# Four PSUM banks in turn, and one signal for two visits, in the segment sum of a graph layer

## What is computed

```python
msg = x @ M
agg = jax.ops.segment_sum(msg[edge_src], edge_dst, num_segments=x.shape[0])
return jax.nn.relu(self_term + agg)          # self_term = x @ W
```

```python
for ei in range(NUM_EXPERTS):
    g = jnp.where(topk_i == ei, w, 0.0).sum(-1)
    hh = jax.nn.gelu(x @ W1[ei] + b1[ei], approximate=False)
    out = out + g[..., None] * (hh @ W2[ei] + b2[ei])
```

## Time and profile before

| | |
|---|---|
| median of 3 runs | 3789.97 us (3778.11 to 3791.41) |
| profiled execution | 3802.64 us, its span 3801.4 us |
| mean granted clock of TensorE | 0.858 of full |
| busy: PE, DVE, ACT, POOL | 71%, 57%, 24%, 62% of the span |
| visits (first to last run) | 82.7 to 2567.2 us |

### The profile page before, as it was taken

How to read it: one execution, slowest core, us unless ns; L and a number is a source line. 1 busy time by engine, 2 the same in 40 slices (tenths; PEclk the granted TensorE clock), 3 DMA queues, 4 the chain that set the end, 5 groups by cost and what they waited for, 6 DMA issues and landing times. The chain is left out here.

```text
span 3801.4 us, 43857 instructions
## 1 busy us (share of the span) xinstructions
PE 2712.7 (71%) x13434; PEld 1990.1 (52%) x13459; DVE 2182.1 (57%) x5820; ACT 905.1 (24%) x1563; POOL 2350.9 (62%) x2748
## 2 busy tenths in 40 slices
PE   2566768777777777687777788776279877788935
PEld 1344545555445554455555555554158755566834
DVE  5777666766755554644554555542014756666857
ACT  3001111111112222111111111111024544444623
POOL 4666666666666666566666666666882678877140
PEclk9767989889888888889898989887668989999968
DMA  9686666666656666566666666663013111211146
GB/s 294 210 255 196 185 201 185 203 188 191 197 181 200 188 200 192 174 203 193 202 208 193 195 206 201 210 177 85 16 13 115 53 37 31 50 50 52 42 138 214
DMA packets 476808, 601.25 MB, mean 158 GB/s; under 512 B 72486, under 2 KB 415390, under 8 KB 474526
## 3 DMA queue, kind: packets, MB, share of 16 engines
q1 hardware_dynamic: 378766, 375.94, 30.4%
q0 software_dynamic: 97216, 219.88, 21.2%
q10 hardware_dynamic: 592, 2.64, 0.2%
HBM read 313.06 MB, written 286.79 MB: 158 GB/s over the span
## 5 line engine op out<-in xcount | busy, mean ns | idle before, releaser
L1705 POOL DMA_INDIRECT ring<-xn_d,srci x1611 | 1565.1, 971 | 928.2 <-DVE ring L820 426.3
L820 DVE SCALAR_TENSOR_TENSOR ring<-ring,same_v,wide 128x256 f32<-128x256 f32 x1610 | 770.6, 479 | 967.0 <-remote 443.0
L1507 PE MATMUL wide<-ring,one_hot 128*128 128x256 f32 x3222 | 980.9, 439 | 478.4 <-DVE ring L820 346.1
L1507 PEld LDWEIGHTS wide<-ring,one_hot 128*128 128x128 f32 x3222 | 659.8, 217 | 756.7 <-DVE ring L820 337.2
L1613 PE MATMUL wide<-tab_parts,low_hot 128*128 128x208 bf16 x6288 | 701.9, 265 | 152.3 <-issue 103.7
L1613 PEld LDWEIGHTS wide<-tab_parts,low_hot 128*128 128x128 bf16 x6288 | 575.0, 102 | 279.5 <-issue 215.1
L1743 POOL DMA_INDIRECT g<-tab_d,srt x500 | 491.8, 984 | 82.2 <-issue 80.6
L1565 PE MATMUL wide<-w2s,hh 128*128 128x256 f32 x1568 | 427.6, 422 | 49.7 <-issue 45.0
L1555 PE MATMUL wide<-xt,w1s 128*128 128x512 f32 (+1 forms) x832 | 416.9, 629 | 34.8 <-issue 17.5
L1240 ACT ACTIVATE hh<-wide,b1c 128x512 f32<-128x512 f32 (+1 forms) x208 | 137.7, 662 | 1177.6 <-PE wide L1555 518.8
L1565 PEld LDWEIGHTS wide<-w2s,hh 128*128 128x128 f32 x1568 | 337.8, 217 | 121.9 <-issue 56.2
(11 more groups left out here) (370 smaller groups left out, 1856.3 us busy)
## 6 DMA issues: line engine op xcount, KB each, us to landing
run_d<-ring SPq DMA_DIRECT2D x201, 1024.0 KB
ring<-xn_d,srci POOLq DMA_INDIRECT x1611
y_d<-yo SPq DMA_DIRECT2D x196, 128.0 KB
comb<-y_d SPq DMA_DIRECT2D x28, 896.0 KB
low_row<-low_d SPq DMA_DIRECT2D x13, 1024.0 KB
sum_d<-g SPq DMA_DIRECT2D x15, 768.0 KB, 4.0
g<-tab_d,srt POOLq DMA_INDIRECT x500
xn_d<-ring SPq DMA_DIRECT2D x7, 896.0 KB, 6.9
```

The source lines that it names most:

```text
L820: dve_at["run", j] = step(V.scalar_tensor_tensor(out=o, in0=ring[:, (j - 1) // JC % RING, (j - 1) % JC, :], scalar=same_v[:, j:j + 1], in1 ...
L1507: T.matmul(wide[:, 4 + j // 2 % 2, j % 2 * D:(j % 2 + 1) * D], one_hot[:, j // 4 % 4, j % 4, :], ring[:, j // JC % RING, j % JC, :], start ...
L1705: G.indirect_dma_start(out=ring[:, s, j % JC, :], out_offset=None, in_=xn_d, in_offset=at_rows(srci[:, j:j + 1])).then_inc(sem(f"gather{s} ...
```

## The change

From pair `wide_from` on, (973 + 13) // 2 = 493 and so visit 986, pairs take the banks 4, 5, 2, 3 in turn; the sort and the search are through with banks 2 and 3 by then. A table says for each pair which earlier pair used its bank last, and TensorE waits for that pair's second run; the first use of banks 2 and 3 waits for the search's last copies out of them (`low_rows`). In all pairs, those before 493 too, only the second visit raises `visited`, and VectorE waits for it before the first run of a pair alone.

```diff
+WIDE_LAG = 13
...
+    PAIRS = -(-V_ // 2)
...
+    wide_from = (sort_end + WIDE_LAG) // 2
+    pair_bank = [4 + p % 2 if p < wide_from else (4, 5, 2, 3)[(p - wide_from) % 4] for p in range(PAIRS)]
+    pair_ahead = [max([q for q in range(p) if pair_bank[q] == pair_bank[p]], default=-1) for p in range(PAIRS)]
...
-                V.wait_ge(sem("visited"), min(j // 2 * 2 + 2, V_))
-                o, more = ring[:, c % RING, j % JC, :], wide[:, 4 + j // 2 % 2, j % 2 * D:(j % 2 + 1) * D]
+                if j % 2 == 0:
+                    V.wait_ge(sem("visited"), j // 2 + 1)
+                o, more = ring[:, c % RING, j % JC, :], bank[pair_bank[j // 2]][:, j % 2 * D:(j % 2 + 1) * D]
...
-            if j >= 4 and j % 2 == 0:
-                T.wait_ge(dve_step, dve_at["run", j - 3])
-            T.matmul(wide[:, 4 + j // 2 % 2, j % 2 * D:(j % 2 + 1) * D], one_hot[:, j // 4 % 4, j % 4, :],
-                     ring[:, j // JC % RING, j % JC, :], start=True, stop=True).then_inc(sem("visited"), 1)
+            p = j // 2
+            if j % 2 == 0 and pair_ahead[p] >= 0:
+                T.wait_ge(dve_step, dve_at["run", 2 * pair_ahead[p] + 1])
+            elif j % 2 == 0 and p >= wide_from:
+                T.wait_ge(dve_step, dve_at["low_rows"])
+            mm = T.matmul(bank[pair_bank[p]][:, j % 2 * D:(j % 2 + 1) * D], one_hot[:, j // 4 % 4, j % 4, :],
+                          ring[:, j // JC % RING, j % JC, :], start=True, stop=True)
+            if j % 2 or j == V_ - 1:
+                mm.then_inc(sem("visited"), 1)
```

## The result

The changed kernel took 3770.09 us in the median of 20 runs (3753.48 to 3787.12), the kernel before 3791.78 us beside it. The ratio is 0.9941, 95% interval 0.9924 to 0.9958: faster by 0.59%, 22 us, where 97 us were forecast. The profiled execution has a span of 3767.3 us, the one before 3801.4 us.

A forecast was written before the change was run, and what follows sets the result against it. The second stage (visits after sort and row search, from 1614 us) was taken as bound by circular waits, with no engine full. -93 - 7 + 3 = -97 us from 3802.6, less 12.6 for the median: 3693 us, range 3605 to 3782.

The forecast's parts named there:

- What bounds the kernel: Visits' time comes out of the end one for one; without a full engine, waits of TensorE, VectorE and GpSimd bind.
- Four banks, -93 us: From visit 986, TensorE waits for the pair four back; 0.65 of its 143.5 us of bank waits saved.
- The wait for yo: Units of kind y share bank 1 and wait for VectorE's yo; in the shown turn this left 0.68 of 2.30 us.
- The late signal: TensorE's signal, some 5 us after the matmul's modelled end, was said to cost nothing with eight visits under way.
- Nothing moves: Rival: the late signal holds the circle, TensorE waits elsewhere for it, only small terms stay; 3786 us, chance 0.13.
- the rival with a wait in the removed one's place: Behind the freed bank waits the unit y stops TensorE, share 0.30 at every pair; 3743 us, chance 0.22.
- bank waits that are gone at an unchanged pace: Sign that the prediction is wrong, which would make the late signal the bound.
- Pair signals, -7 us: One wait fewer before each odd run, 0.06 us a pair, over 118 first-stage waits; dropped signals priced at nothing.
- The seam, +3 us: Where four banks begin, TensorE waits once for VectorE to free bank 4: 2.3 us, +3 us with the restart.
- Clock, 0: The second stage's granted clock, 0.90 of full, should not fall with less idle time; counted as nothing.
- the slower rival: TensorE waits for a chunk's gathers; gain gone at 1.24 us a chunk, 3818 us at 1.6; chance 0.08.
- The rule of the second buffer: A skill page's kernel gained nothing further from a second PSUM buffer; set aside because TensorE stopped for banks 70 times.

The follow-up runs named there:

- e8: The changed kernel without the odd visits' gathers from the fifth chunk on, GpSimd kept busy by three memsets for each; 0.8743 of the kernel before.
- e3: The changed kernel with GpSimd allowed to issue gathers 20 runs ahead instead of 14; 1.0052 of the kernel before.
- e11: The changed kernel with a semaphore for each half of a chunk, so TensorE waits for four gathers instead of eight; 0.9923 of the kernel before.
- e7: The changed kernel without the gathers of the odd visits from the fifth chunk on; 0.8379 of the kernel before.
- e10: The changed kernel with gathers of 64 rows instead of 128 from the fifth chunk on, as many gather instructions; 1.0000 of the kernel before.
- e1: The kernel before with one signal per pair of visits and its two banks kept; 0.9985 of the kernel before.
- e16: The changed kernel with a semaphore for each half chunk and the four banks in the order 2, 3, 5, 4; 0.9924 of the kernel before.
- e2: The changed kernel with a signal and a wait for every visit, its four banks kept; 0.9994 of the kernel before.
- e14: Four banks with a signal for every visit, measured once more beside the whole change on one chip; 0.9964 of the kernel before.
- e9: The changed kernel with a small memset on GpSimd ahead of each gather; 1.0028 of the kernel before.
- run 1139: Not a follow-up run: VectorE's half of visit 1139 in the kernel before; TensorE goes on right behind it at 1848.67 us.
- e5: The changed kernel with half of the matmuls of every MLP unit left out; 0.9832 of the kernel before.

## Why the prediction was wrong in size

- **What bounds the kernel.** Right that time out of the visits comes out of the end one for one, and that no engine is full. The circle was read too early as a circle through the banks: the earlier trace rows names three waiting engines, and the sum rested on the smallest of the three sums.
- **Four banks, -93 us.** This is the step that failed: 0.65 of TensorE's 143.5 us of bank waits, on the ground that GpSimd's 1.25 us would allow it. The waits went entirely; the stage gave 20 us in the profile, and four banks alone 0.06% and 0.36% in two measurements. "What comes next behind the wait that goes" was answered with GpSimd's time for a gather (e8 shows that its time is not the limit) and with yo, but not with the 395 us for which VectorE itself waited for TensorE. These waits, with those whose releaser the profile does not show, stayed (416 and 417 us), and in e3 and e11 the taking away of TensorE's own stops, wherever they are, gained nothing that shows. The wait for yo that the sum looked at did come, at 27.5 us.
- **The late signal.** The rival "Nothing moves" had the mechanism, at a chance of 0.13 and with 3786 us; the measured 3770 lies between it and the rival with a wait in the removed one's place (3743). It was put down with the sentence that a signal 5 us late costs nothing when eight visits are under way. That treats lateness as a fixed delay behind each matmul. The rows show another thing: in the turn after, two pairs are run at once when the signal comes, and how long it takes goes by the gathers (e7, e8, e10). More pairs in flight would then only make the bunch larger. The prediction named the mark of this case itself, "bank waits that are gone at an unchanged pace"; that is nearly what came (1.50 us a visit instead of 1.53).
- **Pair signals, -7 us.** The odd run does start 0.04 us behind the even one instead of 0.10 (two runs take 1.00 us in one row, 1.06 in the earlier trace rows). The first stage got 2.5 us shorter and e1 0.15% faster, both too small to tell from nothing or from 7 us. For the second stage the sum held this part within the bank waits; in VectorE's account it is the part that changed (38.7 to 19.4 us of short gaps), though e1 shows that it comes back as waiting when the banks are two. By the Trainium skill ("TensorE: Matmul & The Clock Gate", section "The cost: per-tile semaphore tail") an estimated 21 us could have come of the dropped increments; e1, 6 us faster by the ratio and between 17 us faster and 6 us slower by its interval, does not show them.
- **The seam, +3 us.** 14 visits at 1.75 us instead of 1.35 make 5.7 us, and e16 gets most of it back in its profile.
- **Clock, 0.** Right: 0.90 in both.
- **Gathers that come late (the slower rival).** TensorE's waits for gathers did grow, from 15.7 to 73.5 us, 0.9 us a chunk and near the price at which the rival decides. But they stand where TensorE has nothing to lose, as e11 shows, so the price was wrong in the same way as the main term.
- **The rule of the second buffer.** The Trainium skill ("TensorE: Matmul & The Clock Gate", section "HAM oscillation — how this bites in real kernels") reports no further gain from a second PSUM buffer in its kernel. This case agrees for the most part: doubling four visits' room to eight gave 0.06% and 0.36% here (e2, e14).

## What to carry to other kernels

A wait that a buffer causes is worth only what the next wait in its circle leaves. Before pricing it, take the longest waits of the same circle and ask whether the freed engine would meet them too; here VectorE waited 395 us for TensorE against TensorE's 143 for VectorE, 416 with the waits of no shown releaser, and with the whole change these were 417. When a signal is late by varying times and several arrive together, look for what runs while they are held (here trains of gathers) and vary its number, size and spacing apart from each other, before adding room to run ahead.

## What the runs showed of the hardware

- TensorE's signals came 9.3 us (a pair of e3) and 28.7 us (the end of e9) behind the modelled end of the matmul while GpSimd issued one indirect DMA behind another. A signal of VectorE in such a turn was not late: in the earlier trace rows TensorE goes on 0.06 us behind the end of run 1139. The Trainium skill ("Perfetto Trace Analysis", section "Tensor Engine Instruction (MATMUL, LD_WEIGHTS)") says that this end is an estimate and that the semaphore update follows only once PSUM has acknowledged the writes. That allows a signal behind the end shown; no figure there comes near 9 us, and no run here shows whether the matmul, its writes or the signal is what waits.
- The effect goes by gather instructions: half of them gave 0.838 of the time of before, a quarter of the bytes 0.995 and half of the rows 1.000. The hold is not complete: at the start of e3 the first three pairs were run between 83.60 and 87.99 us, in the middle of a train of gathers.
- A longer lead for the gathers, with nothing else changed, made both kernels slower, by 0.6% and, from the changed kernel, 1.1%.
- The granted clock of the second stage was 0.90 after the change, 1.00 (the 2.4 GHz level throughout) with half of the gathers, where TensorE was busy 644 of 675 us (e7), and 0.82 (a mix with the 1.2 GHz level) with half of the unit work, where it was busy 630 of 926 us (e5).

Open: how a gather instruction holds TensorE's signals, whether other indirect DMAs of GpSimd do so as well (the end of e9 alone speaks for it), and whether wider gaps between gathers would let them through; a spacing that is really wider than 1.29 us with all gathers kept was not tried.
